# Local attention: the projection of the values moves ahead of those of the queries and keys, and its copy ahead of the exponentials

## The reference

```
h = shift_token(x)                       # half the channels come from the token before
q, k, v = split(h @ wqkv, 3)             # 3 x 512 columns: 8 heads of 64
q = l2norm(q) * qs;  k = l2norm(k) * ksc
q, k = rotary_xpos(q, k)                 # t*cos + swapped(t)*sin, from tables
# windows of 64 tokens: each sees its own window and the one before
attn = softmax(where(mask, -max, (8 q) @ k^T))
o = attn @ v
x = x + o @ wo
```

## Time and profile before

| | us |
|---|---|
| median of 3 runs | 1759.63 (1756.43 to 1762.3) |
| the profiled execution | 1758.3 |
| its span, first to last instruction | 1756.5 |
| first layer's attention stage, about | 376 to 930 |
| second layer's attention stage, about | 1060 to 1610 |
| mean granted TensorE clock over the span | 0.988 |

### The profile page before, as it was taken

How to read it: one execution, slowest core, us unless ns; L and a number is a source line. 1 busy time by engine, 2 the same in 40 slices (tenths; PEclk the granted TensorE clock), 3 DMA queues, 4 the chain that set the end, 5 groups by cost and what they waited for, 6 DMA issues and landing times. The chain is left out here.

```text
span 1756.5 us, 53292 instructions
## 1 busy us (share of the span) xinstructions
PE 1667.7 (95%) x17605; PEld 1151.3 (66%) x17605; DVE 1445.2 (82%) x3283; ACT 1301.4 (74%) x3588; POOL 1038.0 (59%) x1015
## 2 busy tenths in 40 slices
PE   6999999979999999999989997999999999998997
PEld 4666666646767766766765664776776766775664
DVE  3777777779899899899967776899899899895996
ACT  5888888838989899899872225989989989895221
POOL 1333333337777777777763224777777777774664
PEclk9999999989999999999999998999999999998999
DMA  3211111111111111111123321111111111113443
GB/s 112 69 48 48 48 48 48 43 43 35 43 45 33 42 45 34 43 43 36 42 56 90 91 71 40 39 41 42 39 39 42 40 37 42 41 35 85 110 122 86
DMA packets 201094, 93.74 MB, mean 53 GB/s; under 512 B 82578, under 2 KB 192060, under 8 KB 201020
## 3 DMA queue, kind: packets, MB, share of 16 engines
q1 hardware_dynamic: 201020, 92.80, 20.1%
HBM read 50.74 MB, written 25.23 MB: 43 GB/s over the span
## 5 line engine op out<-in xcount | busy, mean ns | idle before, releaser
L847 ACT ACTIVATE pr<-banks,nb,rr 128x128 f32<-128x128 f32 x1024 | 455.2, 463 | 4.8 <-DVE nb L916 4.7
L748 POOL TENSOR_TENSOR rr<-ss,half_neg 128x16 f32<-128x16 f32 x128 | 374.2, 2923 | 19.0 <-POOL ss L745 17.0
L765 POOL TENSOR_TENSOR pr<-pr,rl 128x512 f32<-128x512 f32 x256 | 266.1, 1040 | 100.7 <-DVE rl L878 100.7
L886 DVE TENSOR_REDUCE ss<-sq 128x16 f32<-128x1024 f32 x128 | 156.1, 1219 | 76.5 <-ACT sq L796 63.0
L1220 ACT ACTIVATE f_g<-banks,b_s 128x512 f32<-128x512 f32 (+1 forms) x96 | 65.8, 686 | 203.2 <-PE banks L1304 192.2
L847 ACT ACTIVATION_READ_ACCUMULATOR pr<-banks,nb,rr 128x1 f32 x1024 | 214.9, 210 | 0.0
L987 PE MATMUL banks<-wqkv_s,hT 128*128 128x512 f32 x256 | 143.8, 644 | 24.8 <-ACT sq L831 16.7
L894 DVE TENSOR_REDUCE mx<-banks 128x8 f32<-128x1024 f32 x128 | 156.0, 1219 | 6.7 <-PE banks L1027 6.3
L384 POOL TENSOR_SCALAR a_ve<-a_mv 128x2 f32<-128x2 f32 x96 | 21.2, 221 | 226.6 <-DVE a_mv L395 223.5
L756 POOL TENSOR_TENSOR krot<-ka,rr 128x512 f32<-128x512 f32 x128 | 134.2, 1048 | 22.4 <-POOL rr L748 11.7
L975 PE MATMUL banks<-ident,pr 128*128 128x128 f32 x1024 | 140.9, 280 | 5.9 <-POOL pr L765 5.9
(11 more groups left out here) (126 smaller groups left out, 4174.4 us busy)
## 6 DMA issues: line engine op xcount, KB each, us to landing
ve<-vt SPq DMA_DIRECT2D x128, 128.0 KB, 2.2
hs<-y_d SPq DMA_DIRECT2D x128, 64.0 KB, 2.0
yt<-y_d SPq DMA_DIRECT2D x64, 128.0 KB, 2.1
y_d<-yn SPq DMA_DIRECT2D x64, 128.0 KB, 2.0
f_h<-y_d SPq DMA_DIRECT2D x128, 64.0 KB, 2.0
f_y<-y_d SPq DMA_DIRECT2D x64, 128.0 KB, 2.2
xa<-in_L_attn_x SPq DMA_DIRECT2D x32, 128.0 KB, 2.2
xr<-in_L_attn_x SPq DMA_DIRECT2D x32, 128.0 KB, 2.3
```

Source lines behind the costliest of these rows:

```text
L748: nc.gpsimd.tensor_tensor(rr[:, r, :], ss[:, r, :], half_neg[:], ALU.pow).then_inc(T["rr"], 1)
L765: nc.gpsimd.tensor_tensor(pr[:, e], pr[:, e], rl[:, e].unsqueeze(2).broadcast_to([P, UH, P]), ALU.mult).then_inc(T[("ne", "no")[e]], 1)
L847: a = nc.scalar.activation(pr[:, e, j, :], bank[e][:, j * P:(j + 1) * P], ACT.Exp, bias=nb[:, X.t, UH * e + j:UH * e + j + 1], scale=rr[:, ...
L886: nc.vector.tensor_reduce(ss[:, 2 * X.p + X.t, :], sq[:].rearrange("p (h d) -> p h d", d=DH), AX.X, ALU.add).then_inc(T["ss"], 1)
```

## The change

Three things go together. The values of a tile are projected first of the three projections of a slot, right behind the turned probabilities; they go into bank 6 + X.t, which held the tile's own queries, and wait only for the squares of those. ScalarE copies them right behind the turned probabilities, ahead of the first four exponentials. The keys' projection of the next tile, which goes into the same bank, now waits for that copy (`until(pe, T["v"], X.x)`). The two waits at the seams between stages move along.

```
 def v_bank(X):
-    return bank[7 - X.t]
+    return bank[6 + X.t]
...
 def t_act(act, l, i, p, s):
     weighed(Tile(l, i, p, s, 4))
     turned_even(Tile(l, i, p, s, 3))
     turned_odd(Tile(l, i, p, s, 3))
+    values(Tile(l, i, p, s, 1))
     exps(Tile(l, i, p, s, 2), 0)
     squares_q(Tile(l, i, p, s, 0))
     exps(Tile(l, i, p, s, 2), 1)
     turned_k(Tile(l, i, p, s, 1))
     squares_k(Tile(l, i, p, s, 0))
-    values(Tile(l, i, p, s, 1))
...
 def project_v(X):
-    passed_tile(pe, T["qs"], X, 1)
-    if at(X, 0):
+    pe.wait_ge(T["qs"], X.x + 1)
+    if at(X, 1):
...
 def scores(X):
     until(pe, T["po"], X.x)
+    if at(X, 0):
+        pe.wait_ge(T["qs"], X.x + 2)
...
 def project_k(X):
-    until(pe, T["v"], X.x - 1)
+    until(pe, T["v"], X.x)
...
     turn_even(Tile(l, i, p, s, 3))
     turn_odd(Tile(l, i, p, s, 3))
+    project_v(Tile(l, i, p, s, 1))
     project_q(Tile(l, i, p, s, 0))
     project_k(Tile(l, i, p, s, 0))
     turn_q(Tile(l, i, p, s, 1))
     out_project(Tile(l, i, p, s, 4))
-    project_v(Tile(l, i, p, s, 1))
     turn_k(Tile(l, i, p, s, 1))
```

## The result

| | before | after |
|---|---|---|
| median, us | 1759.91 (4 runs) | 1793.03 (4 runs, 1791.52 to 1794.78) |
| ratio | 1 | 1.019, 95% interval 1.017 to 1.021 |
| span of the profiled execution | 1756.5 | 1793.0 |
| a slot of the attention stage | 8.204 | 8.474 |

What follows compares the result with a forecast made beforehand. Bound: a loop of waits through minus peak, exponentials, squares, key copy, key squares and sums, 8.20 us a slot. The new loop's terms sum to 8.45, +0.25 over 120 slots, +30 us: 1788, range 1775 to 1805.

Steps and rivals of the forecast that it cites:

- side branch: TensorE's 0.35 us wait before the values' projection was said to hang off the bounding loop, not lie on it.
- (1) TensorE: Values projected right behind the turned probabilities: the 0.35 us wait goes, and the pair takes 1.02 instead of 1.12.
- TensorE's case: Rival: TensorE is the bound, so closing its gap returns 0.35 us a slot, 42 us, giving 1716; chance 8%.
- (2) The bank: Values and the next tile's keys share a bank; the keys' projection waits 0.03 us for the copy, hidden, costing 0.
- (3) The queries' projection: It comes 0.86 us later on TensorE; VectorE's `m1q` starts 1.97 after the values' start, the squares can start at 3.29.
- near tie: Squares of the queries could start at 3.29 by VectorE's `m2q`, against 3.33 by ScalarE's copy and exponentials.
- much slower rival: The later queries' projection holds VectorE, squares start late, exponentials stretch: 8.77 us a slot, +68 us, 1827; chance 13%.
- (4) ScalarE, the sum: The value copy ahead of the exponentials closes a new loop through key copy, scores and values' projection: 8.45 us a slot.
- Loops B and C: Not in the prediction: ways through key squares and GpSimd's norms to the keys' turning, over two slots and one slot.
- loop A: The predicted one-slot loop: key copy, scores, turnings, values, value copy, exponentials, squares, exponentials, key copy; 8.45 us.
- The count of slots, 120: 60 slots a layer were counted in the attention stages, 120 in all, each +0.25 us, for +30 us.
- The expected signs: ScalarE's copy waits 0.3 to 0.5 us, `nb` ready early, scores 0.69 after key copy with TensorE idle, `m1q` waits.

Runs made afterwards that it cites:

- e1: The kernel before, with a second copy of the values bank into a spare tile at ScalarE's end of the slot; 1756.85 us, ratio 0.9996.
- e12: The kernel before, with GpSimd's power split into two halves of 8 columns, the keys' first; 1753.94 us, ratio 0.9986.
- e8: The kernel before, with GpSimd's power replaced by one short product of constant tiles, inverse norms left out; 1834.62 us, ratio 1.0447.
- e10: The changed kernel, squares of the queries behind the key copy, rotated keys scaled by a constant ahead of GpSimd's power; 1758.53 us, ratio 1.0009.
- e13: The kernel before, with only ScalarE's value copy moved, one slot later and ahead of the exponentials, TensorE's order untouched; 1786.78 us, ratio 1.0173.
- e3: The changed kernel, with the squares of the queries behind the key copy instead of between the two groups of exponentials; 1797.26 us, ratio 1.0229.
- e5: The changed kernel, with GpSimd's power replaced by one short product of constant tiles, inverse norms left out; 1829.79 us, ratio 1.0419.
- e6: The changed kernel, with the short product for GpSimd's power and the squares of the queries behind the key copy; 1800.67 us, ratio 1.0254.
- e11: The changed kernel, squares of the queries behind the key copy, GpSimd's power in two halves, the keys' first; 1763.95 us, ratio 1.0048.

## Why the prediction was right

- **What bounds the kernel.** The loop from minus peak over the squares of the queries, the key copy and the sums, with the value copy outside: e1 doubles the copy and nothing moves. e12 leaves GpSimd out of it, e8 shows that `nb` is in it. Two of its links were read a little wrong. From `nb` to the squares it runs through VectorE's rotations, as the prediction says where it reads `m2q`; the first four exponentials have 0.2 us to spare and are not in it. And from the squares to the key copy there are two ways of nearly one length, ScalarE's own, and TensorE's through the projection of the values and the turning of the keys. The second is the longer one. Of the trace of before, ScalarE's squares of the queries and its last exponential, then TensorE's projection of the values:

```profile
486.71 0.60 ACT L831 ACTIVATE sq<-banks 128x512 f32<-128x512 f32 x1
...
488.51 0.47 ACT L847 ACTIVATE pr<-banks,nb,rr 128x128 f32<-128x128 f32 x1
```

```profile
487.36 1.12 PE L987 MATMUL banks<-wqkv_s,hT 128*128 128x512 f32 x2
```

  Squares 486.71, values 487.36, turning 488.32, key copy 489.03: 2.32. ScalarE alone would have been ready 0.44 after its last exponential, at 488.95. In the 49 slots from 450 to 850 us the key copy starts 0.45 to 0.53 after the last exponential, 0.51 on average, and after the change 0.44. So TensorE's wait was no pure side branch: about 0.07 us of its 0.35 lay on the loop.
- **(1) TensorE.** The 0.35 us wait and the longer pair went, as said, and the kernel got slower. TensorE's case (1716, 8%) did not come, and by these rows it could have brought back 0.07 x 128 = 9 us at most, not 42. TensorE's part of the change by itself was not run. The section Identifying the Most-Contended Engine of the Trainium skill, Perfetto Trace Analysis, which was put in its favour, does not judge TensorE by the busy share of its matmuls but by the share of the peak that it reaches and by the busy share of the weight loads, here 66%; so the 95% alone did not make this its case.
- **(2) The bank.** 0.03 us was forecast for the wait of the keys' projection. It starts 1.78 after the values' (488.01 to 489.79) against 1.72 unhindered, 0.06, and its pair takes 1.13 instead of 1.02 with an exposed weight load, 0.11 which I had left out. The 0.70 us of the weight unit in the waits is not time that TensorE loses. 0.17 in all, and hidden: the turning of the keys further down TensorE's queue waits 0.30 for GpSimd all the same, and e10 has these waits and 1758.53 us. In e13, where the copy comes later against the keys' projection, the same wait sets the slot. The rule of the Trainium skill, Perfetto Trace Analysis, section Optimizing Tensor Performance (Matmuls), on rotating the banks would have put its price on the sum; the trace shows the wait, but off the path.
- **(3) The queries' projection.** `m1q` was to start 1.97 after the values' projection and started 1.93 after it (488.01 to 489.94); `m2q` ended 1.28 later, at 491.22, and the squares were issued at 491.38. The near tie held, with 0.16 to spare, and the much slower rival (1827) did not come.
- **(4) ScalarE, the sum.** Forecast 8.45, measured 8.474. Term by term: key copy to scores 0.73 (0.69), scores 1.21 (1.21), turnings 0.93 (0.93), projection to copy 1.07 to 1.14 (1.11), copy 0.48 (0.46), exponentials 1.75 (1.80), squares 0.48 (0.49), exponentials 1.75 (1.76).
- **What was missed.** Loops B and C. They were left out of the sum, though their terms were in the trace of before. B ends within 0.05 us of loop A, so the time would have come out the same by it, and C is 0.38 shorter. It was luck that neither is longer than A. It would not have come out for anyone who went on from the forecast: loop A alone promised 0.49 us a slot for moving the squares (e3), and loop C took it all. The count of slots, 120, was a little low: 33.1 / 0.270 = 123 from the medians, 135 from the two spans.
- **The expected signs.** The exponentials behind the copy with `nb` 0.6 us old, ScalarE's wait for the projection (0.28, said 0.3 to 0.5), and `m1q` waiting came; an idle TensorE ahead of the scores hardly shows (0.16 us in one slot, none in the next), since the turning of the keys, which waits for GpSimd, and the weighing behind it fill TensorE's queue until the key copy is done.

## What to carry to other kernels

Closing a gap of the busiest engine pays only for the part of the gap that no other way of the same loop covers, here 0.07 of 0.35 us. Before a copy is moved, ask whether it stands in idle time now and which instructions will queue behind it, and count its full pitch (from its start to the next one's) if one of them is on the loop. When a loop is found, look for the next ones within a few per cent before you promise a gain from shortening it, and ask of each move which other loop it makes longer: e3 took the squares out of one loop and put them into another. When a run comes out as forecast, still look which of its waits were closed; e13 gave the number by another way than the changed kernel. A test that takes work off one engine also moves what that engine does next, so check the durations of its neighbours first.

## What the runs showed of the hardware

- VectorE's `nb`, 8 elements a partition, took 0.76 to 0.95 us instead of 0.17 when issued under a running product of GpSimd of 128 x 512 elements, and ended 0.01 to 0.03 us after it, in all 137 slots of e5, e6 and e8 from 450 to 850 us.
- GpSimd's power takes 1.64 to 1.67 us for 8 columns (e11) and 2.92 for 16: about 0.16 us a column and 0.4 at the start. One of 4 columns in another stage of the kernel before takes 1.03.
- ScalarE's recorded durations changed with its schedule while the distances between starts hardly did: the copy of turned h is 298 ns before and 327 after, the key copy 0.59 and 0.63, and from the key copy to the next start it is 0.48 and 0.47. Sums were better made from start to start.
